# Turning the halves of heads on VectorE's shuffle instead of by TensorE products, in a four-part cross-attention kernel

## The reference

```python
def rotate_half(x):
    d = x.shape[-1] // 2
    return jnp.concatenate([-x[..., d:], x[..., :d]], axis=-1)

def apply_rotary(q, k, position_ids, seq_len):
    inv = 1.0 / 10000.0 ** (jnp.arange(0, HD, 2, dtype=jnp.float32) / HD)
    freqs = jnp.outer(jnp.arange(seq_len, dtype=jnp.float32), inv)
    emb = jnp.concatenate([freqs, freqs], axis=-1)
    cos = jnp.cos(emb)[position_ids][:, None].astype(q.dtype)
    sin = jnp.sin(emb)[position_ids][:, None].astype(q.dtype)
    return (q * cos + rotate_half(q) * sin, k * cos + rotate_half(k) * sin)

x = rms_norm(hidden_states, ln_in_w)
mixed = jnp.where(vm, x @ v_qkv, x @ l_qkv)
q, k, v = jnp.split(mixed, 3, axis=-1)
q, k, v = (heads(q, NH, HD), heads(k, NH, HD), heads(v, NH, HD))
q, k = apply_rotary(q, k, position_ids, l)
ctx = sdpa(q, k, v, causal=True)
```

## Time and profile before

| | us |
|---|---|
| median of 3 runs | 748.28 |
| lowest and highest | 746.57 and 749.37 |
| profiled execution | 751.68 |
| its span, first to last instruction | 749.9 |
| PE busy | 678.5 (90%) |
| PE weight loads busy | 538.6 (72%) |
| DVE busy | 400.0 (53%) |
| ACT busy | 352.7 (47%) |
| POOL busy | 109.0 (15%) |

### The profile page before, as it was taken

The page is one execution under the profiler, slowest core; times in us unless marked ns, Lnnn a source line. Parts: engine busy times, 40 slices in busy tenths (PEclk is TensorE's granted clock), DMA queues, the critical chain, the costliest instruction groups (busy, mean ns, idle before and its releaser), DMA issues.

```text
span 749.9 us, 13217 instructions
## 1 busy us (share of the span) xinstructions
PE 678.5 (90%) x5514; PEld 538.6 (72%) x5514; DVE 400.0 (53%) x805; ACT 352.7 (47%) x711; POOL 109.0 (15%) x140
## 2 busy tenths in 40 slices
PE   5997997879999999999889979979799989999995
PEld 4885765548897777778768767755598967776984
DVE  2739537555574555341455684383685374645315
ACT  4522452477352666553434225526473236575424
POOL 0100000480000332200001000007600004132000
PEclk9997999698999999999989969968899999999998
DMA  8132001022004000050400200000120400000000
GB/s 291 64 152 85 2 1 30 1 78 78 1 1 169 1 2 1 1 190 1 183 28 1 77 9 2 2 29 12 68 78 1 168 1 2 1 2 1 0 1 28
DMA packets 6843, 34.54 MB, mean 46 GB/s; under 512 B 1537, under 2 KB 3073, under 8 KB 5249
## 3 DMA queue, kind: packets, MB, share of 16 engines
q1 hardware_dynamic: 5344, 26.85, 9.7%
q10 hardware_dynamic: 1440, 6.86, 2.5%
HBM read 32.66 MB, written 1.05 MB: 45 GB/s over the span
## 4 chain that ended last, share of the span: by engine, by line
PE 75%; DVE 14%; ACT 7%; issue 2%; DMA 1%; POOL 1%; SPq 0%; DVEq 0%; ACTq 0%; POOLq 0%
PE ps_A L733 5%; PE ps_B L952 4%; PE ps_A L952 4%; PE ps_B L733 3%; PE ps_A L915 3%; PE ps_B L915 3%; PE ps_A L1029 3%; PE ps_B L1029 3%; PE ps_B L1079 2%; PE ps_A L1079 2%; PE ps_A L748 2%; PE ps_A L1108 2%; PE ps_B L748 2%; PE ps_A L1067 2%; PE ps_B L863 2%
## 5 line engine op out<-in xcount | busy, mean ns | idle before, releaser
L562 POOL TENSOR_TENSOR xv_A<-big_A 128x256 f32<-128x256 f32 x24 | 18.0, 756 | 215.8 <-ACT big_A L1386 113.6
L562 POOL TENSOR_TENSOR xv_B<-big_B 128x256 f32<-128x256 f32 x24 | 18.5, 776 | 205.2 <-ACT big_B L1386 102.8
L1726 DVE TENSOR_REDUCE max_B<-ps_B 128x2 f32<-128x512 f32 x64 | 40.4, 685 | 14.7 <-PE ps_B L878 9.7
L1726 DVE TENSOR_REDUCE max_A<-ps_A 128x2 f32<-128x512 f32 x64 | 40.0, 685 | 13.9 <-PE ps_A L878 7.2
L1203 ACT ACT_TABLE_LOAD x31 | 39.8, 1283 | 0.5
L733 PE MATMUL ps_A<-q_A,kz_A 128*128 128x256 f32 x264 | 36.8, 300 | 3.2 <-DVE q_A L1617 3.2
L733 PEld LDWEIGHTS ps_A<-q_A,kz_A 128*128 128x128 f32 x264 | 34.7, 203 | 4.9 <-DVE q_A L1617 3.4
L733 PE MATMUL ps_B<-q_B,kz_B 128*128 128x256 f32 x264 | 36.7, 299 | 1.1 <-DVE kz_B L1638 1.1
L733 PEld LDWEIGHTS ps_B<-q_B,kz_B 128*128 128x128 f32 x264 | 34.7, 203 | 2.7 <-issue 2.4
L915 PE MATMUL ps_A<-q_A,kz_A 64*128 64x256 f32 (+1 forms) x320 | 32.7, 317 | 3.7 <-ACT big_A L1390 2.2
L1390 ACT ACTIVATE big_B<-ps_B 128x384 f32<-128x384 f32 (+1 forms) x48 | 23.7, 543 | 23.8 <-PE ps_B L926 23.7
(11 more groups left out here) (413 smaller groups left out, 1651.5 us busy)
## 6 DMA issues: line engine op xcount, KB each, us to landing
ffn_w<-in_l1m SPq DMA_DIRECT2D x2, 3072.0 KB, 11.1
ffn_w<-in_l2f SPq DMA_DIRECT2D x2, 3072.0 KB, 10.3
attn_w<-in_l1a SPq DMA_DIRECT2D x2, 2048.0 KB, 9.2
v_B<-in_l1d ACTq DMA_DIRECT2D x2, 1408.0 KB, 6.8
v_A<-in_l1d ACTq DMA_DIRECT2D x2, 1408.0 KB, 6.4
attn_w<-in_l2q SPq DMA_DIRECT2D x2, 1024.0 KB, 5.1
attn_w<-in_l2q SPq DMA_DIRECT2D x4, 512.0 KB, 4.9
v_A<-in_gm SPq DMA_DIRECT2D x2, 512.0 KB, 5.8
```

The lines of the kernel that those rows point to most:

```text
L562: nc.gpsimd.tensor_tensor(L.key_sums(a, i), p[:, 0:S], p[:, S:2 * S], ALU.add)\
L1726: last = nc.vector.tensor_reduce(mx[:, :, h], L.ps[:, h % 4, :].rearrange("p (q k) -> p q k", q=ST), AX.X, ALU.max)
```

## The change

`rotate_halves`, `qk_save` and the matrix `rot` are gone. The signs are now in the table of sines. DVE brings the halves of heads across by `stream_shuffle` within each group of 32 partitions, straight from PSUM, and also takes the cosine product straight from PSUM. Queries (j = 0) and keys (j = 1) go through rotation, rounding and low part apart, 512 columns each. `self_qkv` makes values first, then queries, then keys. `stack_self` waits for each of the two by itself, and in addition for DVE to have read both from PSUM (`qk_read`). SP's transfer of the next weights waits for the keys in place of the values. The four tables of `ORDER` are new throughout.

```diff
-(K_IDENT, K_ONES, K_ROT, K_IOTA, K_EPS, K_SUM16, K_SUM8, K_END) = columns(P, P, P, 1, 3, 48, 56)
+(K_IDENT, K_ONES, K_IOTA, K_EPS, K_SUM16, K_SUM8, K_END) = columns(P, P, 1, 3, 48, 56)
+OTHER_HALF = [r + 8 if r % 16 < 8 else r - 8 for r in range(32)]
...
 ORDER = {
     "PE": [
-        0, 1, 2, 1, 1, 1, 2, 3, 2, 1, 1, 2, 4, 2, 3, 8, 5, 1, 2, 1, 1, 5, 1, 3, 1, 1, 1, 1, 2, 1, 2, 3, 2,
+        0, 1, 2, 1, 1, 1, 2, 3, 2, 1, 1, 2, 4, 2, 3, 7, 3, 1, 3, 1, 1, 2, 1, 6, 1, 1, 1, 1, 2, 1, 1, 3, 2,
...
                 for L in lanes:
-                    sp.wait_ge(*L.v_done.at(it, 1))
+                    sp.wait_ge(*L.qk_done.at(it, 2))
...
+                    if it == 0 and L.t == 0:
+                        pe.wait_ge(trig_ready.sem, 1)
+                    for kt in range(ST):
+                        for i, (at, src, c) in enumerate(parts):
+                            if kt == 0 and i == DC:
+                                yield
+                                pe.wait_ge(*L.split.at(it, 1))
+                            last = mm(L.half(3, kt), L.chunk(src, c, kt * P, (kt + 1) * P),
+                                      w(attn_w, at, c, 2 * D, 3 * D, 3 * D), start=(i == 0), stop=(i == 3))
+                        if kt == ST - 1:
+                            last.then_inc(L.v_done.sem, 1)
+                        yield
                     for m in range(4):
...
-                def rotate_halves(L):
-                    pe.wait_ge(*L.qk_saved.at(it, 2))
-                    for m in range(4):
-                        last = mm(L.half(m // 2, m % 2), rot, L.chunk(L.big, m), start=True, stop=True)
-                    last.then_inc(L.rot_done.sem, 1)
-                    yield
...
-                    pe.wait_ge(*L.hi_ready.at(it, 1))
-                    pe.wait_ge(*L.lo_ready.at(it, 1))
+                    pe.wait_ge(*L.qk_read.at(it, 2))
                     pe.wait_ge(*L.v_saved.at(it, 1))
                     for what, (hi, lo) in enumerate(((Q_HI, Q_LO), (K_HI, K_LO))):
                         if what:
                             pe.wait_ge(*L.q_ready.at(it, 4))
+                        pe.wait_ge(*L.hi_ready.at(it, what + 1))
+                        pe.wait_ge(*L.lo_ready.at(it, what + 1))
...
-                def qk_save(L):
+                def self_hi(L):
+
                     for j in range(2):
-                        act.wait_ge(*L.qk_done.at(it, j + 1))
-                        fn(L.big[:, j * 512:(j + 1) * 512], L.ps[:, j, :], ACT.Copy)\
-                            .then_inc(L.qk_saved.sem, 1)
+                        act.wait_ge(*L.rotated.at(it, j + 1))
+                        fn(L.parts[:, j * 512:(j + 1) * 512], L.big[:, 1024 + j * 512:1024 + (j + 1) * 512], ACT.Copy)\
+                            .then_inc(L.hi_ready.sem, 1)
                         yield
...
-                def rotate(L):
+                def rotate(L, j):
 
                     if it == 0:
                         dve.wait_ge(trig_ready.sem, 1)
-                    dve.wait_ge(*L.qk_saved.at(it, 2))
-                    tt(lines(L.big2[:, 0:1024], 4), lines(L.big[:, 0:1024], 4), spread(cos[:], 4), ALU.mult)
-                    yield
-                    dve.wait_ge(*L.rot_done.at(it, 1))
-                    step.done(tt(lines(L.big2[:, 1024:2048], 4),
-                                 L.ps[:, 0:2, :].rearrange("p b (n s) -> p (b n) s", s=S), spread(sin[:], 4),
-                                 ALU.mult))
-                    last = tt(L.big[:, 1024:2048], L.big2[:, 0:1024], L.big2[:, 1024:2048], ALU.add)
-                    last.then_inc(L.rotated.sem, 1)
-                    yield
+                    dve.wait_ge(*L.qk_done.at(it, j + 1))
+                    other, plain, turned = (tile[:, at + j * 512:at + (j + 1) * 512]
+                                            for tile, at in ((L.big, 0), (L.big2, 0), (L.big2, 1024)))
+                    nc.vector.stream_shuffle(other, L.ps[:, j, :], OTHER_HALF)
+                    tt(lines(plain, 2), lines(L.ps[:, j, :], 2), spread(cos[:], 2), ALU.mult)\
+                        .then_inc(L.qk_read.sem, 1)
+                    dve.wait_ge(*L.qk_read.at(it, j + 1))
+                    step.done(tt(lines(turned, 2), lines(other, 2), spread(sin[:], 2), ALU.mult))
+                    tt(L.big[:, 1024 + j * 512:1024 + (j + 1) * 512], plain, turned, ALU.add)\
+                        .then_inc(L.rotated.sem, 1)
+                    yield
...
+                def self_lo(L, j):
+
+                    dve.wait_ge(*L.hi_ready.at(it, j + 1))
+                    at = j * 512
+                    tt(L.parts[:, 1024 + at:1536 + at], L.big[:, 1024 + at:1536 + at],
+                       L.parts[:, at:at + 512].bitcast(F32), ALU.subtract).then_inc(L.lo_ready.sem, 1)
                     yield
...
-                yield from rotate(L)
-                yield from self_lo(L)
+                for j in range(2):
+                    yield from rotate(L, j)
+                    yield from self_lo(L, j)
```

More of the change, by code:

```diff
@@ L276, in __init__ @@
                 self.w_lo = s("w_lo", IC + 2)
-                self.hi_ready = s("hi_ready", 3)
-                self.lo_ready = s("lo_ready", 3)
+                self.hi_ready = s("hi_ready", 4)
+                self.lo_ready = s("lo_ready", 4)
                 self.q_stacked = s("q_stacked", 2)
@@ L283, in __init__ @@
                 self.qk_done = s("qk_done", 2)
-                self.qk_saved = s("qk_saved", 2)
-                self.rot_done = s("rot_done")
-                self.rotated = s("rotated")
+                self.qk_read = s("qk_read", 2)
+                self.rotated = s("rotated", 2)
                 self.cross_done = s("cross_done", 2)
@@ L420, in build @@
         ones = const[:, K_ONES:K_ONES + P]
-        rot = const[:, K_ROT:K_ROT + P]
         identb = constb[:]
@@ L744, in self_qkv @@
                         for i, (at, src, c) in enumerate(parts):
-                            if m == 0 and i == DC:
-                                yield
-                                pe.wait_ge(*L.split.at(it, 1))
                             last = mm(L.half(m // 2, m % 2), w(attn_w, at, c, m * P, (m + 1) * P, 3 * D),
@@ L752, in self_qkv @@
                         yield
-                    if it == 0 and L.t == 0:
-                        pe.wait_ge(trig_ready.sem, 1)
-                    for kt in range(ST):
-                        for i, (at, src, c) in enumerate(parts):
-                            last = mm(L.half(3, kt), L.chunk(src, c, kt * P, (kt + 1) * P),
-                                      w(attn_w, at, c, 2 * D, 3 * D, 3 * D), start=(i == 0), stop=(i == 3))
-                        if kt == ST - 1:
-                            last.then_inc(L.v_done.sem, 1)
-                        yield
-                def rotate_halves(L):
-                    pe.wait_ge(*L.qk_saved.at(it, 2))
-                    for m in range(4):
-                        last = mm(L.half(m // 2, m % 2), rot, L.chunk(L.big, m), start=True, stop=True)
-                    last.then_inc(L.rot_done.sem, 1)
-                    yield
                 def cross_keys_and_values(L):
@@ L790, in stack_cross_keys @@
                 def stack_cross_keys(L):
-                    pe.wait_ge(*L.hi_ready.at(it, 2))
-                    pe.wait_ge(*L.lo_ready.at(it, 2))
+                    pe.wait_ge(*L.hi_ready.at(it, 3))
+                    pe.wait_ge(*L.lo_ready.at(it, 3))
                     pe.wait_ge(*L.v_saved.at(it, 2))
@@ L820, in stack_cross_queries @@
                 def stack_cross_queries(L):
-                    pe.wait_ge(*L.hi_ready.at(it, 3))
-                    pe.wait_ge(*L.lo_ready.at(it, 3))
+                    pe.wait_ge(*L.hi_ready.at(it, 4))
+                    pe.wait_ge(*L.lo_ready.at(it, 4))
                     place_blocks(L, CROSS, Q_HI, Q_LO, lambda part: L.chunk(L.cross_parts, 2 + part),
@@ L1137, in batch @@
                 yield from self_qkv(L)
-                yield from rotate_halves(L)
                 yield from stack_self(L)
@@ L1452, in batch @@
                     yield from rotary_tables(L)
-                yield from qk_save(L)
                 yield from self_hi(L)
@@ L1683, in cross_key_lo @@
                 def cross_key_lo(L):
-                    dve.wait_ge(*L.hi_ready.at(it, 2))
+                    dve.wait_ge(*L.hi_ready.at(it, 3))
                     tt(L.chunk(L.cross_parts, 1), L.half(0, 0), L.chunk(L.cross_parts, 0).bitcast(F32),
@@ L1870, in tables @@
     const[:, K_ONES:K_ONES + P] = 1.0
-    for r in range(P):
-        j = r % dim
-        const[r + dim // 2 if j < dim // 2 else r - dim // 2, K_ROT + r] = -1.0 if j < dim // 2 else 1.0
     trig = np.zeros((P, T_END), f)
-    for at, table in ((T_COS, np.cos(emb)), (T_SIN, np.sin(emb))):
+    sign = np.where(np.arange(dim) < dim // 2, f(-1.0), f(1.0))
+    for at, table in ((T_COS, np.cos(emb)), (T_SIN, np.sin(emb) * sign)):
         spread = table[:, rows % dim]
```

13 lines of the change are left out of this document (2 added, 11 removed), and 42 rows, old and new, of the table ORDER.

## The result

The change takes 743.51 us as the median of 12 executions (lowest 741.72), the kernel before beside it 746.50. The ratio is 0.9951, with a 95% interval of 0.9929 to 0.9973: 0.5% faster, at the edge of what I had called measurable. The forecast was 742.0 us, in a range from 736.5 to 747.5. One of the twelve executions took 1527.93 us, for a reason that no row shows: the ratio leaves it out, and without it the median is 743.14. The profiled execution took 744.03 us, with a span of 742.2 us, 7.7 less than the span before.

A forecast was written before the change was run, and what follows sets the result against it. In each pair's stage TensorE was taken as the bound first, then DVE. Gains of 3.2 and 2.9 us in the stages and 0.2 in loads, 6.3 in all, off the 748.28 median gave 742.0 us, range 736.5 to 747.5.

The forecast's parts named there:

- The two stages: First pair 32.0 to 73.8 us, second 402.28 to 443.81, each TensorE's then DVE's: 3.2 and 2.9 us shorter.
- The shuffle: On DVE in the rotation of queries and keys: 0.72 us per 128x512 with its gap, bounded by 0.53 and 1.38.
- The load of the constants: At the start, queued ahead of lane B's input: 64 KB less, 0 to 0.9 us, taken as 0.2.
- From the median: 742.0: Whole kernel: 6.3 us taken off the median of 748.28 us, though the profiled execution took 751.68.
- the 0 for all that lies outside the stages: Rest of the program: same operations, interleaved a little otherwise, worth 0, give or take 2 us.
- the new interleaving costs a clock fall elsewhere: Rival, outside the stages: one more half-clock stretch of TensorE costs about 4 us, giving 746.0; chance 0.22.
- The stretch I named: 131 to 140 us, where TensorE ran at 0.53 of full clock, the example for the interleaving rival.
- The sign that the prediction gave for the interleaving: The gain at 74 us, where the first stage ends, would be gone by 250 us.
- the clock does not fall: Rival, behind both stages (74 to 78, 444 to 446 us): full clock kept, 3.0 us more, 739.0; chance 0.12.
- slow shuffle: Rival, on DVE in the stages: 2.76 us a shuffle, each pair losing 4.1 us, 756.3; loss from about 1.75; chance 0.05.
- TensorE's busy time: Sign over the whole kernel: TensorE's busy time should fall by some 7 us.

The follow-up runs named there:

- the filled kernels: Kernel before and changed kernel, each with 18 unread filler products between the pairs: 746.20 us for before; 740.04 and, in a second series, 742.43 us for the change.
- before again: The kernel before, unedited, run and traced a second time: median 748.53 us, ratio 1.0009 to the kernel before.
- change again: The changed kernel, unedited, run and traced a second time: median 743.88 us, ratio 0.9921 to the kernel before.

## Why the prediction was right or wrong

**The two stages: right, somewhat undersized.** The forecast was 3.2 and 2.9 us. Measured are 3.5 to 3.8 and 4.0. The mechanism is the one given: the first lane's products off TensorE's full stretch (1.31 and 1.73 us a stage when tried alone, 1.65 and 1.74 up to the first scores, 1.73 forecast), and DVE's work of the second stretch brought forward. First scores at 55.26 (forecast 55), first maximum at 58.38 (58.5), A's scores at 70.83 (70.6). The second pair was under-read: I gave it 38.6 us as its stage, and it took 37.57. I had carried the first pair's count over without working it out. The first pair's 38.34 is itself part clock. There PEclk from 55.26 to 70.83 is 0.63, and the second execution's stage took 38.00.

**The shuffle: right.** 0.72 us was taken, 0.73 is measured, 0.77 from one shuffle to the next and 0.63 to a product behind it. The prediction's estimate from the figure of the Trainium skill ("VectorE: DVE Perf Modes", "The perf-mode tier table") was 0.80 at 512 columns, a little above. The rule of the same page of the Trainium skill to keep chained DVE operations few ("Rules for kernel authors") is borne out on the path alone: the shuffles away gave 0.8 to 0.9 us a pair, twice the shuffles cost 1.7 to 2.0, about half of it in the stretch where DVE sets the end. As a whole the change goes against it, from 4 chained steps to 10, and the stages became shorter by 3.5 to 4.0 us.

**The load of the constants: 0.2 us, not to be seen.** The stage starts at 30.0 to 32.5 us in fourteen traces without order: 31.1 as the mean of four traces of before and its variants, 31.3 of the change's ten. The transfers at the start scatter by more than the term: TensorE's wait for B's input is 1.5 and 0.4 us in the two traces of before, 1.0 and 1.8 in those of the change.

**What was mis-sized: "From the median: 742.0", and the 0 for all that lies outside the stages.** The measured time lies 1.5 us from the forecast, and part of that closeness is luck: the stages gave 1.3 to 1.7 us more than forecast, and other places took more than that back. I took 6.3 off a median as if all executions of the kernel had the clock falls of the one that I read. That execution was of the upper kind, with a fall between the pairs. Half or more of before's executions seem to go without it: 26 of 46 are of the lower kind, whose one trace has none. The change has it in each of its traces. By the table: with the fall in both (before and change), 7.7 us less, of which the stages are 7.4. With it in neither (the filled kernels), 8.3 to 9.2, of which the stages are 7.7; "between" is 1.7 to 1.9 us longer and "rest" 2.4 to 2.5 shorter. With it in the change alone (before again and change again), 1.6, though the stages are 7.8: "between" is 4.1 us longer, the start 1.1 later and "rest" 0.9 longer. Of the 4.1, 2.6 lie behind the mark near 330 us, most of it the gap's fall (2.2 by the fillers), and 1.5 ahead of it, where only the order of turns is new. The prediction had put 0 outside the stages, give or take 2, and a clock fall as a rival. The median of before is a mixture of the two kinds, and the change stands at 2.5 us below the lower (746.0) and 7.4 below the upper (750.9).

**The rival "the new interleaving costs a clock fall elsewhere": partly what happened**, in a place where I had not looked. Its chance of 0.22 was argued down by the lack of a new wait; the fall came in a gap where before has it too, in one of its two traces. The stretch I named did get its clock back, and others fell. The sign that the prediction gave for the interleaving, the gain of 74 us gone by 250, did not come as such: against before again the change again is 2.7 us ahead at its stage's end and still 1.2 ahead at the mark near 330 us. In the changed kernel:

```profile
71.00:75.00 4.00, 4.00 (x38) 0.50 0.02 4
...
131.00:140.00 9.00, 7.99 (x112) 1.00 0.01 2
```

From 131 to 140 us it is 1.00 where it was 0.53. At 375 to 380 it is 0.50, and in the second pair's cross attention 0.51 to 0.56 from 520 to 530. The first of these two rows settles the rival **"the clock does not fall"**: behind the DVE-bound stretch the clock is at half speed as before. The **slow shuffle** did not happen (0.73 us against the 1.75 from which it would decide).

**TensorE's busy time** fell by 4.2 us and not by 7. The 16 products are gone. Against before again (676.7 us busy) it is even 2.4 only: what the falls at half clock add to other products is in the same sum, so the busy time could not show the step.

## What to carry to other kernels

Moving work from a full engine to one with idle time pays when the receiving engine can start on the first part while the rest is still being made. Here the same operations cost 1.4% in one piece and gained 0.5% in two. Before taking a sum off a median, look whether the execution that was read belongs to the median's kind: compare its time with the spread of the runs, and its clock row by row with a second trace. Where the order of the whole program is new, "outside the stage nothing changes" is a term of its own: cut the span at marks that both programs have, and compare stretch by stretch. Where TensorE idles in a gap between stages and its clock is at half behind it, a few products that nobody reads are a cheap trial.

## What was not expected of the hardware

The same kernel had two traces with the same order of instructions in the gap between the pairs, and the granted clock fell in one (0.50 of full speed from 380 to 385 us) and not in the other (1.00). 18 filler products there kept it at 1.00 in every trace. By the means of their executions the change with them is 2.2 us faster (743.0 in its second series without, 740.8 with, on another chip) and the kernel before 2.0 (748.2 and 746.3), though they are work added. The later half-clock stretches shifted with the earlier ones: with the gap's fall gone, the change's window at 520 to 530 us was at 1.00 instead of 0.56. That one fall brings another 150 us later is how I read this; it was not tried by itself, and the kernel before speaks against a general rule: with and without the gap's fall its "rest" is 306.1 and 305.3 us. Which property of the gap decides was not tried either.
